# Shared expert weights in pieces of 256, 256 and 192 columns: the last 64 columns of gate and up as one chunk

## The chip, the cores and the metric

The kernel runs on one core of a Trainium2 chip. The metric is the device time of one execution in microseconds; three executions of the kernel before gave 2449.96, 2451.63 and 2456.68 us.

## The reference

A transformer block on 8192 tokens of 256 numbers (8 sequences of 1024), in float32:

```python
xn = _layernorm(x, axis=-1)
x = x + attention(xn) + ffn(xn)          # 16 heads of 16, ALiBi bias, softmax over the keys

# ffn: 8 experts of width 352, the best two of each token; one shared expert of width 704
h = jax.nn.silu(jnp.einsum('tc,ech->eth', xf, W1)) * jnp.einsum('tc,ech->eth', xf, W2)
y = jnp.einsum('eth,ehc,te->tc', h, W3, w)
hs = jax.nn.silu(xf @ Ws1) * (xf @ Ws2)
y = y.reshape(b, t, c) + (hs @ Ws3).reshape(b, t, c)
```

The shared expert is what the change is about: gate `xf @ Ws1` and up `xf @ Ws2`, each 256 to 704, their product `hs`, and down `hs @ Ws3`, 704 back to 256, for every token.

## The kernel before, in words

A float32 product is made of three matmuls on numbers split in a high part (rounded by a cast to fp32r) and a low part (what is left): low by high, high by low, high by high (`mm3`). All matmuls of this kind stand on one line, L497.

Each engine has a class (`Tensor`, `Scalar`, `Vector`, `Pool`, `Sync`) with the same methods, and `Order.run` calls them in one order for all. So the order of an engine is written out by hand, and engines meet at semaphores. The program has four stages: norm and projections; attention (with the routing, and transfers on POOL's queue that pack each expert's weights into a DRAM tensor `Wd`, `pack_expert`); 71 blocks (NBLK) of 256 routed rows, each with the weights of its expert; and 16 groups (NG) of 512 tokens with the shared expert, the attention's output projection and the sum of everything.

The shared expert is treated as two more experts of width 352. `pack_expert` packs them as experts 8 and 9, and `gather_weights` loads them as blocks 71 and 72 into one of three raw buffers WR (b % 3) with one transfer of 128 rows of 2176 numbers each. `split_block(b, i)` then splits three pieces of a set of weights: ACT casts all three to the high part (L806), POOL makes the low part of piece 0 (L1286), DVE that of pieces 1 and 2 (L1054). In a group, `shared_up(g, x, hc)` makes one of six chunks: two halves x of the width, each in chunks hc of 128, 128 and 96 columns. A chunk is 6 matmuls of gate and 6 of up, on PE, with 512 tokens as moving columns. Then ACT makes silu of gate (L848), DVE multiplies by up (`hf`, L1100), ACT casts that to the high part (`HH`, L854) and DVE makes the low part (`HL`, L1103).

A group's order on PE is: chunk 0, then the former group's `shared_down`, chunks 1, 2 and 3, the transposes of the next group's tokens (`group_columns`, L510; ACT and DVE turn them into high and low columns, L836 and L1083), chunks 4 and 5. `shared_down` has 24 matmuls of the attention's output with Wo and 72 on the six chunks, for four column blocks of 128 tokens. In the first group `shared_up(0, 0, 0)` stands before the last expert block's `block_down`, and the weights of the second half are split just behind it.

The waits that matter here: a gate chunk waits for the silu of the chunk two before it (`sg`), an up chunk for its product (`hf`), each chunk for the split weights (`wslp` by POOL, `wslv` by DVE) and for the group's columns (`sch`, `scl`). A load into WR[b % 3] waits until the set before in that buffer is split, a split into WB[b % 3] until the block before in it has done its down part (`down`).

Of the kernel before, what the change touches and what calls it, by code (L numbers as in the profile page):

```python
# [32 lines left out]
PIECES = ((0, W2_AT), (W2_AT, W3_AT), (W3_AT, RAW))  # L33
SCALE = float(HD) ** -0.5
# [43 lines left out]
class Order:  # L78
# [3 lines left out]
    def run(self):  # L82
# [96 lines left out]
        self.shared_up(0, 0, 0)  # L179
        self.block_down(NBLK - 1)  # L180
        for i in range(3):
            self.split_block(NBLK + 1, i)
        for j in range(4):
            self.gather_rows(0, j)
        for g in range(NG + 1):
            if 0 < g < NG:
                self.shared_up(g, 0, 0)
            if g >= 1:
                self.shared_down(g - 1)
            if g < NG:  # L190
                self.shared_up(g, 0, 1)
                self.o_columns(g)
                self.shared_up(g, 0, 2)
            if 1 <= g < NG:
                self.load_res(g)
                for j in range(4):
                    self.gather_rows(g, j)
            if g < NG:
                if g + 1 < NG:
                    self.load_o(g + 1)  # L200
                self.shared_up(g, 1, 0)
                if g + 1 < NG:
                    self.group_columns(g + 1)
                self.shared_up(g, 1, 1)
                self.shared_up(g, 1, 2)
                if g + 2 < NG:
                    self.load_rows(g + 2)
        self.end()

    def attention(self, s, n):  # L210
# [25 lines left out]
        if r % 2 == 0 and r // 2 < NE + 2 and kc == 1:  # L236
            self.pack_expert(r // 2)
# [65 lines left out]
    def shared_up(self, g, x, hc): pass  # L303
# [29 lines left out]
def up_index(g, x, hc):  # L333
    return NUP + 6 * g + 3 * x + hc


def build(nc, t, out):
    ctx = ExitStack()
    with ctx:
# [16 lines left out]
        Wd = dram("Wd", [(NE + 2) * P, RAW])  # L356
# [135 lines left out]
        class Tensor(Order):  # L492
# [194 lines left out]
            def shared_up(self, g, x, hc):  # L687
                h0, hn = HC[hc]
                n = up_index(g, x, hc)
                k, wt = (NBLK + g) % 2, WB[(NBLK + x) % 3]  # L690
                banks = 2 + 2 * (n % 2), 3 + 2 * (n % 2)
                self.w.wait_ge("sch", NBLK + g + 1)
# [5 lines left out]
                self.mm3(ps[0:hn, banks[0], :], self.operands(CH[:, k, :, :], CL[:, k, :, :], wt, h0, hn)  # L698
                         ).then_inc(sem["gmm"], 1)
                self.w.wait_ge("hf", n - 1)  # L700
                self.mm3(ps[0:hn, banks[1], :], self.operands(CH[:, k, :, :], CL[:, k, :, :], wt, W2_AT + h0, hn)
                         ).then_inc(sem["up"], 1)

            def shared_down(self, g):
                self.w.wait_ge("wslv", 2 * (NBLK + 2))
# [9 lines left out]
                for j in range(4):  # L715
                    col = slice(j * P, (j + 1) * P)
                    ks = []
                    for x in range(2):
                        wt = WB[(NBLK + x) % 3]
                        for hc in range(3):  # L720
                            n, hn, a = up_index(g, x, hc), HC[hc][1], W3_AT + hc * D
                            self.w.wait_ge("hh", n + 1)
                            self.w.wait_ge("hl", n + 1)
                            ks.append((HH[0:hn, n % 8, col], HL[0:hn, n % 8, col],
                                       wt[0:hn, a:a + D], wt[0:hn, RAW + a:RAW + a + D]))
                    self.mm3(ps[:, 6 + j // 2, (j % 2) * D:(j % 2) * D + D], ks, False, j % 2 == 1
                             ).then_inc(sem["sdn"], 1)


        class Scalar(Order):  # L730
# [65 lines left out]
            def split_block(self, b, i):  # L796
                if b > NBLK + 1:
                    return
                lo, hi = PIECES[i]
                self.w.wait_ge(f"wb{b % 3}", 16 * (b // 3 + 1))  # L800
                self.w.wait_ge("down", b - 2)
                if b in (1, 2):
                    self.w.wait_ge("acc1", NPAIR)
                    self.w.wait_ge("zero", 16 * NBLK)
                    self.w.wait_ge("wd", 80 * (NE + 2))
# [37 lines left out]
            def shared_up(self, g, x, hc):  # L843
                hn, n = HC[hc][1], up_index(g, x, hc)
                s, k = n % 8, n % 2
                self.w.wait_ge("hf", max(n - 1, NUP))
                self.w.wait_ge("gmm", n - NUP + 1)
                self.e.activation(sg[0:hn, k, :], ps[0:hn, 2 + 2 * (n % 2), :], ACT.Silu).then_inc(sem["sg"], 1)  # L848
# [5 lines left out]
                self.e.copy(HH[0:hn, s, :], hf[0:hn, k, :]).then_inc(sem["hh"], 1)  # L854


        class Vector(Order):
# [190 lines left out]
            def split_block(self, b, i):  # L1048
                if b > NBLK + 1 or i == 0:
                    return  # L1050
                lo, hi = PIECES[i]
# [40 lines left out]
            def shared_up(self, g, x, hc):  # L1092
                e = self.e
                hn, n = HC[hc][1], up_index(g, x, hc)
# [5 lines left out]
                e.tensor_tensor(hf[0:hn, k, :], ps[0:hn, 3 + 2 * (n % 2), :], sg[0:hn, k, :], ALU.mult  # L1100
                                ).then_inc(sem["hf"], 1)
                self.w.wait_ge("hh", n + 1)
                e.tensor_tensor(HL[0:hn, s, :], hf[0:hn, k, :], HH[0:hn, s, :].bitcast(F32),  # L1103
                                ALU.subtract).then_inc(sem["hl"], 1)
# [28 lines left out]
        class Pool(Order):  # L1133
# [89 lines left out]
            def pack_expert(self, x):  # L1223
                e = self.e
                if x < NE:
                    w1, w2, w3 = t["W1"][x], t["W2"][x], t["W3"][x]
                else:
                    a = (x - NE) * HE
                    w1, w2, w3 = t["Ws1"][:, a:a + HE], t["Ws2"][:, a:a + HE], t["Ws3"][a:a + HE, :]
# [34 lines left out]
            def gather_weights(self, b):  # L1264
                k = b % 3
                if b < NBLK:
                    self.w.wait_ge("rtw", 1)
                    self.w.wait_ge("wd", 80 * (NE + 2))
# [5 lines left out]
                else:  # L1274
                    e0 = (NE + b - NBLK) * P
                    self.w.wait_ge("wslp", b - 2)
                    self.w.wait_ge("wslv", 2 * (b - 2))
                    self.e.dma_start(WR[k][:, :], Wd[e0:e0 + P, :]).then_inc(sem[f"wb{k}"], 16)

            def split_block(self, b, i):  # L1280
                if b > NBLK + 1 or i != 0:
                    return
                lo, hi = PIECES[0]
# [22 lines left out]
            def shared_down(self, g):  # L1306
# [3 lines left out]
                self.w.wait_ge("hl", up_index(g + 1, 0, 0))  # L1310
# [213 lines left out]
```

## Time and profile before

| what | us |
|---|---|
| median of 3 executions | 2451.63 |
| lowest, highest | 2449.96, 2456.68 |
| the profiled execution | 2450.59 |
| its span | 2448.5 |
| busy in the span: PE, DVE, ACT, POOL | 2410.8, 2014.0, 1714.1, 1042.4 |
| first group's chunk 0 starts on PE at | 1975.13 |

Times of rows are microseconds from the start of the span. Between the profiled execution and its span lie 2.1 us outside the profile. PE is the matrix engine, DVE, ACT and POOL the vector, scalar and GpSimd engines, SP the queue that issues most transfers. A busy share counts instructions, and matmuls are pipelined, with modelled ends: the distance between the starts of two rows tells how fast they go, not their printed durations.

### The profile page before, as it was taken

To read this page: it belongs to the slowest core of one execution; us is meant where nothing else is said; L and a number is where in the kernel's file an instruction comes from. 1 tells how busy PE (TensorE), PEld (TensorE's weight loads), DVE (VectorE), ACT (ScalarE), POOL (GpSimd) and SP (SyncE) were. 2 spreads that over 40 slices of the span, in tenths; PEclk is the share of its full clock that TensorE was granted. 3 is DMA by queue.
4 is the path that set the end of the run, shared out by engine and by line. 5 is a ranking of instruction groups with operands and counts; after the bars stand their busy time and mean duration, and the time that the engine had idled before them with its cause. 6 is when DMAs were issued, how large, how long until landed. Compare 5 with 4: busy or idle time off the path is not lost.

```text
span 2448.5 us, 52126 instructions
## 1 busy us (share of the span) xinstructions
PE 2410.8 (98%) x20122; PEld 1605.7 (66%) x20122; DVE 2014.0 (82%) x3277; ACT 1714.1 (70%) x3274; POOL 1042.4 (43%) x994
## 2 busy tenths in 40 slices
PE   7999999999999999999999999999999999999999
PEld 5775444444444444444444448999999988888887
DVE  7987999999999999999999956777777765444444
ACT  4444888888889999998999997777777743332222
POOL 3332454544224545555455324333333334444444
PEclk9996999999999999999999999999999999999999
DMA  8994454544323444344443335777777744433332
GB/s 289 340 321 149 144 165 138 167 150 141 87 79 111 130 122 125 116 117 130 124 124 107 103 97 174 241 237 239 238 238 238 238 142 115 117 109 104 104 104 87
DMA packets 220263, 385.53 MB, mean 157 GB/s; under 512 B 53892, under 2 KB 141124, under 8 KB 210644
## 3 DMA queue, kind: packets, MB, share of 16 engines
q1 hardware_dynamic: 181744, 219.30, 29.2%
q0 software_dynamic: 37184, 162.09, 20.7%
q8 instruction: 160, 2.62, 0.5%
q10 hardware_dynamic: 1088, 0.79, 0.1%
q14 instruction: 87, 0.71, 0.1%
HBM read 250.15 MB, written 142.54 MB: 160 GB/s over the span
## 4 chain that ended last, share of the span: by engine, by line
PE 78%; DVE 18%; issue 3%; ACT 1%; DMA 0%; POOL 0%; DVEq 0%; SPq 0%; ACTq 0%; POOLq 0%
PE ps L497 76%; DVE mx L927 11%; DVE mx L930 4%; PE ps L510 2%; DVE qkL L917 0%; ACT qkH L767 0%; DVE xn L901 0%; DVE stats L866 0%; DMA xr<-Xn 0%; DMA xt<-in_x 0%; DVE XL L909 0%; POOL rstd L1155 0%; DVE mT L940 0%; DVE VB L1071 0%; ACT pta L782 0%
## 5 line engine op out<-in xcount | busy, mean ns | idle before, releaser
L927 DVE TENSOR_REDUCE mx<-ps 128x1 f32<-128x512 f32 x1560 | 964.7, 685 | 19.1 <-PE ps L497 17.7
L497 PE MATMUL ps<-OPS 54*128 54x512 f32 (+1 forms) x4096 | 792.0, 451 | 5.9 <-DVE mx L927 2.6
L497 PEld LDWEIGHTS ps<-OPS 54*128 54x128 f32 (+1 forms) x4096 | 388.6, 186 | 483.3 <-ACT pta L782 195.8
L782 ACT ACTIVATE pta<-ps 128x512 f32<-128x512 f32 x1024 | 541.5, 598 | 110.2 <-PE ps L497 104.7
L782 ACT ACTIVATE ptb<-ps 128x512 f32<-128x512 f32 x1024 | 538.8, 600 | 55.5 <-PE ps L497 48.2
L497 PE MATMUL ps<-OPS,WB 128*128 128x256 f32 (+1 forms) x2268 | 363.5, 312 | 2.9 <-DVE VB L1071 1.5
L497 PEld LDWEIGHTS ps<-OPS,WB 128*128 128x128 f32 x2268 | 310.6, 180 | 32.2 <-issue 3.3
L497 PE MATMUL ps<-pta,VB 128*32 128x352 f32 (+1 forms) x4096 | 304.1, 392 | 0.1
L497 PE MATMUL ps<-ptb,VB 128*32 128x352 f32 (+1 forms) x4096 | 302.4, 390 | 0.0
L930 DVE TENSOR_REDUCE mx<-ps 128x2 f32<-128x1024 f32 x244 | 297.8, 1220 | 0.0
L497 PE MATMUL ps<-OPS,WB0c 128*128 128x256 f32 (+3 forms) x1440 | 257.9, 331 | 2.9 <-DVE VB L1071 1.9
L497 PEld LDWEIGHTS ps<-OPS,WB0c 128*128 128x128 f32 (+1 forms) x1440 | 210.3, 181 | 32.9 <-issue 3.7
L1204 POOL TENSOR_SCALAR m<-m 128x16 f32<-128x16 f32 x64 | 19.3, 301 | 480.2 <-DVE m L934 480.2
L1216 POOL TENSOR_TENSOR sq<-sq,mone 128x16 f32<-128x16 f32 x64 | 190.1, 2971 | 69.4 <-DMA sq<-accs 68.8
L497 PE MATMUL ps<-WB,OPS 128*128 128x256 f32 (+1 forms) x1422 | 188.1, 283 | 0.0
L1076 DVE TENSOR_TENSOR OPS<-VB,OPS 128x256 fp32r<-128x256 f32 (+1 forms) x213 | 151.3, 710 | 33.6 <-ACT OPS L824 33.6
L848 ACT ACTIVATE VB<-ps 128x512 f32<-128x512 f32 (+1 forms) x96 | 57.0, 594 | 174.1 <-PE ps L497 174.1
L497 PEld LDWEIGHTS ps<-WB,OPS 128*128 128x128 f32 (+1 forms) x1422 | 178.4, 191 | 0.1
L497 PEld LDWEIGHTS ps<-ptb,VB 128*32 128x32 f32 x4096 | 94.2, 109 | 118.3 <-issue 116.7
L497 PEld LDWEIGHTS ps<-pta,VB 128*32 128x32 f32 x4096 | 94.2, 109 | 116.0 <-issue 100.2
L1260 POOL DMA_INDIRECT Xs<-xr,slot x128 | 131.1, 1024 | 59.3 <-PE ps L497 53.4
L854 ACT CAST OPS<-VB 128x512 fp32r<-128x512 f32 (+1 forms) x96 | 59.6, 621 | 138.2 <-DVE VB L1100 138.2
(155 smaller groups left out, 3003.1 us busy)
## 6 DMA issues: line engine op xcount, KB each, us to landing
OPS<-QKh SPq DMA_DIRECT2D x512, 64.0 KB
Xs<-zero POOLq DMA_DIRECT2D x71, 256.0 KB, 3.1
xr<-Xs SPq DMA_DIRECT2D x71, 256.0 KB, 5.3
Ys<-VB SPq DMA_DIRECT2D x71, 256.0 KB, 5.0
QKh<-qkH SPq DMA_DIRECT2D x16, 1024.0 KB, 7.2
QKl<-qkL SPq DMA_DIRECT2D x16, 1024.0 KB, 9.0
OPS<-QKl SPq DMA_DIRECT2D x256, 64.0 KB
asum<-Sd SPq DMA_DIRECT2D x64, 256.0 KB
```

What stands on the lines that cost most here:

```text
L497: return self.e.matmul(o, l, r, start=start, stop=stop)
L510: return self.e.transpose(o, in_, ident[:, :])
L782: self.e.activation(pt(m)[:, half * GT:(half + 1) * GT], ps[:, n % 3, :], ACT.Exp).then_inc(sem["exp"], 1)
L848: self.e.activation(sg[0:hn, k, :], ps[0:hn, 2 + 2 * (n % 2), :], ACT.Silu).then_inc(sem["sg"], 1)
L854: self.e.copy(HH[0:hn, s, :], hf[0:hn, k, :]).then_inc(sem["hh"], 1)
L927: self.e.reduce_max(mx[:, r % 2, hh, i, half:half + 1], ps[:, bank, :], AX.X).then_inc(sem["mxred"], 1)
L930: self.e.reduce_max(mx[:, r % 2, hh, i, :], ps[:, bank - 1:bank + 1, :], AX.X).then_inc(sem["mxred"], 2)
L1076: e.tensor_tensor(HL[0:hn, s, 0:BT], hfq[0:hn, k, :], HH[0:hn, s, 0:BT].bitcast(F32), ALU.subtract).then_inc(sem["hl"], 1)
L1204: e.tensor_scalar(m16[:, k2, :, :], m16[:, k2, :, :], -1.0, None, ALU.mult).then_inc(sem["mng"], 1)
L1216: self.e.tensor_tensor(sq[:, :], sq[:, :], mone[:, :], ALU.pow).then_inc(sem["rcp"], 1)
L1260: e.indirect_dma_start(Xs[:, :], bass.IndirectOffsetOnAxis(ap=slot[:, c, 4 * g + j:4 * g + j + 1], axis=0), xr[:, k, j, :], None).then_inc ...
```

## The change

The width 704 is no longer two halves of 352, but 256 + 256 + 192. There are five full chunks of 128 columns, and a sixth that holds the last 64 columns of gate in its rows 0 to 63 and the last 64 of up in rows 64 to 127, so that one set of 6 matmuls makes both. ACT's silu reads rows 0 to 63 and writes 64 to 127, where up and the product are. The sixth chunk's high part lies in rows 64 to 127 and its low part in rows 0 to 63 of one tile (`HH`), and down takes it with 2 matmuls instead of 3: against the low weights (zeros in rows 0 to 63), and against the high weights (the same 64 rows twice). The shared weights are now three sets, blocks 71, 72 and 73. They are not packed, but loaded from the inputs with 3, 3 and 7 transfers, and the third set is split behind the second.

```diff
+SX = 2 * D
+SHARED = (((0, SX), (SX, 2 * SX), (2 * SX, 3 * SX)), ((0, SX), (SX, 2 * SX), (2 * SX, 3 * SX)),
+          ((0, 4 * P), (4 * P, 6 * P), (6 * P, 10 * P)))
+SHARED_LOADS = (3, 3, 7)
...
-            if b + 3 <= NBLK + 1:
+            if b + 3 <= NBLK + 2:
                 self.gather_weights(b + 3)
...
-        self.shared_up(0, 0, 0)
+        self.shared_up(0, 0)
         self.block_down(NBLK - 1)
-        for i in range(3):
-            self.split_block(NBLK + 1, i)
+        for x in (1, 2):
+            for i in range(3):
+                self.split_block(NBLK + x, i)
...
-        if r % 2 == 0 and r // 2 < NE + 2 and kc == 1:
+        if r % 2 == 0 and r // 2 < NE and kc == 1:
             self.pack_expert(r // 2)
...
-        Wd = dram("Wd", [(NE + 2) * P, RAW])
+        Wd = dram("Wd", [NE * P, RAW])
...
+                at, up_at, step = ((j % 2) * P, SX + (j % 2) * P, D) if j < 4 else ((j - 4) * 4 * P, 2 * P, P)
...
+                if j == 1:
+                    self.w.wait_ge("hf", n - 1)
+                gate = self.mm3(ps[:, banks[0], :], self.shared_operands(xh, xl, wt, at, step))
+                if j == 5:
+                    gate.then_inc(sem["up"], 1)
+                else:
+                    gate.then_inc(sem["gmm"], 1)
+                    self.w.wait_ge("hf", n - 1)
+                    self.mm3(ps[:, banks[1], :], self.shared_operands(xh, xl, wt, up_at, step)).then_inc(sem["up"], 1)
...
             def shared_down(self, g):
-                self.w.wait_ge("wslv", 2 * (NBLK + 2))
+                self.w.wait_ge("wslv", 2 * (NBLK + 3))
...
+                    self.mm3(out_j, ks, False, False)
+                    n, wt, a = up_index(g, 5), WB[(NBLK + 2) % 3], 8 * P
+                    self.w.wait_ge("hh", n + 1)
+                    self.w.wait_ge("hl", n + 1)
+                    self.mm(out_j, HH[:, n % 8, col], wt[:, RAW + a:RAW + a + D], False, False)
+                    self.mm(out_j, HH[:, n % 8, col], wt[:, a:a + D], False, j % 2 == 1).then_inc(sem["sdn"], 1)
...
+                    self.w.wait_ge("up", n + 1)
+                    self.e.activation(sg[64:P, k, :], ps[0:64, bank, :], ACT.Silu).then_inc(sem["sg"], 1)
...
+                    self.e.copy(HH[64:P, s, :], hf[64:P, k, :]).then_inc(sem["hh"], 1)
...
+                if b == NBLK + 2 and i == 2:
+                    hi = 8 * P
+                    self.e.tensor_tensor(wt[64:P, RAW + hi:RAW + hi + D], WR[b % 3][64:P, hi:hi + D],
+                                         wt[64:P, hi:hi + D].bitcast(F32), ALU.subtract)
+                    self.e.tensor_scalar(wt[0:64, RAW + hi:RAW + hi + D], WR[b % 3][0:64, hi:hi + D], 0.0, None, ALU.mult)
...
+                    e.tensor_tensor(hf[64:P, k, :], ps[64:P, 2 + 2 * (n % 2), :], sg[64:P, k, :], ALU.mult
+                                    ).then_inc(sem["hf"], 1)
+                    self.w.wait_ge("hh", n + 1)
+                    e.tensor_tensor(HH[0:64, s, :], hf[64:P, k, :], HH[64:P, s, :].bitcast(F32), ALU.subtract
+                                    ).then_inc(sem["hl"], 1)
...
-                    self.e.dma_start(WR[k][:, :], Wd[e0:e0 + P, :]).then_inc(sem[f"wb{k}"], 16)
+                    w1, w2, w3, x, done = t["Ws1"], t["Ws2"], t["Ws3"], b - NBLK, sem[f"wb{k}"]
+                    parts = ((0, 2 * D, D, w1), (SX, 2 * D, D, w2)) if x < 2 else (
+                        (0, 2 * P, P, w1), (2 * P, 2 * P, P, w2), (4 * P, 2 * P, 64, w1), (4 * P + 64, 2 * P, 64, w2))
+                    for i, (at, size, width, w) in enumerate(parts):
+                        c0 = x * D if i < 2 else 5 * P
+                        lo = at if i < 2 else 4 * P
+                        self.e.dma_start(WR[k][:, lo:lo + size].rearrange("p (c n) -> p c n", c=2)
+                                         [:, :, at - lo:at - lo + width], rows(w[:, c0:c0 + width])).then_inc(done, 16)
+                    if x < 2:
+                        self.e.dma_start(WR[k][:, 2 * SX:3 * SX].rearrange("p (c n) -> p c n", c=2),
+                                         rows(w3[x * D:(x + 1) * D, :])).then_inc(done, 16)
+                    else:
+                        self.e.dma_start(WR[k][:, 6 * P:8 * P], w3[4 * P:5 * P, :]).then_inc(done, 16)
+                        for i in range(2):
+                            self.e.dma_start(WR[k][64 * i:64 * i + 64, 8 * P:10 * P], w3[5 * P:5 * P + 64, :]
+                                             ).then_inc(done, 16)
```

How the order changes on PE, in the first group from the last block's down part (WB1) to the attention's projections; WB2 and WB0c are the first and second set, WB1 the third. Before:

```order
L497 MATMUL ps<-WB1,OPS 128x256 x18
L497 MATMUL ps<-OPS,WB2 128x512 x12
L497 MATMUL ps<-OPS,WB2 96x512 x12
L497 MATMUL ps<-OPS,WB0c 128x512 x12
L510 MATMUL ps<-ident,xr 128x128 x8
L497 MATMUL ps<-OPS,WB0c 128x512 x12
L497 MATMUL ps<-OPS,WB0c 96x512 x12
```

Now:

```order
L511 MATMUL ps<-WB1,OPS 128x256 x18
L511 MATMUL ps<-OPS,WB2 128x512 x12
L511 MATMUL ps<-OPS,WB0c 128x512 x24
L524 MATMUL ps<-ident,xr 128x128 x8
L511 MATMUL ps<-OPS,WB1 128x512 x18
```

Chunk 2 belongs to the second set now, where it was the last chunk of the first; behind the transposes stand 18 matmuls instead of 24 up to the next group's chunk 0.

The same engine in `shared_down`, on the six chunks of a group (the last row is the next group's chunk 1). Before:

```order
L497 MATMUL ps<-WB2,OPS 128x256 x9
L497 MATMUL ps<-WB0c,OPS 128x256 x9
L497 MATMUL ps<-WB2,OPS 128x256 x9
L497 MATMUL ps<-WB0c,OPS 128x256 x9
L497 MATMUL ps<-WB2,OPS 128x256 x9
L497 MATMUL ps<-WB0c,OPS 128x256 x9
L497 MATMUL ps<-WB2,OPS 128x256 x9
L497 MATMUL ps<-WB0c,OPS 128x256 x9
L497 MATMUL ps<-OPS,WB2 128x512 x12
```

Now:

```order
L511 MATMUL ps<-WB2,OPS 128x256 x6
L511 MATMUL ps<-WB0c,OPS 128x256 x6
L511 MATMUL ps<-WB1,OPS 128x256 x5
L511 MATMUL ps<-WB2,OPS 128x256 x6
L511 MATMUL ps<-WB0c,OPS 128x256 x6
L511 MATMUL ps<-WB1,OPS 128x256 x5
L511 MATMUL ps<-WB2,OPS 128x256 x6
L511 MATMUL ps<-WB0c,OPS 128x256 x6
L511 MATMUL ps<-WB1,OPS 128x256 x5
L511 MATMUL ps<-WB2,OPS 128x256 x6
L511 MATMUL ps<-WB0c,OPS 128x256 x6
L511 MATMUL ps<-WB1,OPS 128x256 x5
```

Each of the four column blocks has 17 matmuls where it had 18.

DVE in the first group, from chunk 0's two steps over the splits to chunk 1's (WR0c and WR1c are the raw buffers of the second and the third set). Before:

```order
L1100 TENSOR_TENSOR VB<-ps,VB 128x512
L1103 TENSOR_TENSOR OPS<-VB,OPS 128x512
L1054 TENSOR_TENSOR WB0c<-WR0c,WB0c 128x704
L1054 TENSOR_TENSOR WB0c<-WR0c,WB0c 128x768
L1100 TENSOR_TENSOR VB<-ps,VB 128x512
```

Now:

```order
L1140 TENSOR_TENSOR VB<-ps,VB 128x512
L1142 TENSOR_TENSOR OPS<-VB,OPS 128x512
L1093 TENSOR_TENSOR WB0c<-WR0c,WB0c 128x512 x2
L1093 TENSOR_TENSOR WB1<-WR1c,WB1 128x256
L1090 TENSOR_TENSOR WB1<-WR1c,WB1 64x256
L1092 TENSOR_SCALAR WB1<-WR1c 64x256
L1093 TENSOR_TENSOR WB1<-WR1c,WB1 128x256
L1140 TENSOR_TENSOR VB<-ps,VB 128x512
```

Two operations between the steps of chunk 0 and of chunk 1 have become six.

## Rows read from the trace of the kernel before

**Rows 1.** The page's busy times: us, share of the span, instructions.

```profile
PE 2410.8 (98%) x20122; PEld 1605.7 (66%) x20122; DVE 2014.0 (82%) x3277; ACT 1714.1 (70%) x3274; POOL 1042.4 (43%) x994
```

**Rows 2.** Stretch in the shared stage: PE, PEld, DVE, ACT, POOL busy; PEclk, DMA share, GB/s.

```profile
2000.00:2100.00 100.00, 100.00 (x623) 87.73 (x623) 47.85 (x76) 27.21 (x43) 40.75 (x32) 1.00 0.36 95
```

**Rows 3.** The chain of waits: start, length, what. One group and the end.

```profile
2018.83 28.21 PE ps L497 x168
2047.04 0.87 PE ps L510 x8
...
2397.11 45.32 PE ps L497 x288
```

**Rows 4.** Timeline of PE: start, us, engine line op out<-in. One steady group.

```profile
2029.88 1.24 PE L497 MATMUL ps<-WB,OPS 128*128 128x256 f32 x9
...
2038.52 5.72 PE L497 MATMUL ps<-OPS,WB 128*128 128x512 f32 x24
2044.08 2.96 PE L497 MATMUL ps<-OPS,WB0c 128*128 128x512 f32 x12
2046.88 1.03 PE L510 MATMUL ps<-ident,xr 128*128 128x128 f32 x8
2047.67 5.82 PE L497 MATMUL ps<-OPS,WB0c 128*128 128x512 f32 x24
```

**Rows 5.** Groups on POOL in the attention stage: the packing transfers' issue, busy and mean ns.

```profile
L1231 POOL DMA_DIRECT2D Wd<-in_Ws x2 | 1.6, 804 | 0.0
...
L1235 POOL DMA_DIRECT2D Wd<-in_Ws x2 | 1.1, 562 | 0.0
```

**Rows 6.** Timeline of POOL around the first group: the splits.

```profile
1968.49 1.71 POOL L1286 TENSOR_TENSOR WB<-WR2c,WB 128x704 fp32r<-128x704 f32 x1 [4.63 <-ACT WB L806]
1981.74 1.71 POOL L1286 TENSOR_TENSOR WB0c<-WR0c,WB0c 128x704 fp32r<-128x704 f32 x1 [11.54 <-ACT WB0c L806]
```

**Rows 7.** DMA issues by tensor, whole run: count, KB each, median us to landing.

```profile
xr<-Xn SPq DMA_DIRECT2D x16, 512.0 KB, 11.3
...
Wd<-in_Ws POOLq DMA_DIRECT2D x4, 352.0 KB, 3.9
...
WR0c<-Wd POOLq DMA_DIRECT2D x1, 1088.0 KB, 5.6
```

**Rows 8.** Timeline of ACT in the first group: the three casts and what follows.

```profile
1980.88 2.20 ACT L806 CAST WB0c<-WR0c 128x704 fp32r<-128x704 f32 x3
1982.97 0.60 ACT L848 ACTIVATE VB<-ps 128x512 f32<-128x512 f32 x1
```

**Rows 9.** Timeline of PE in the first group: chunks 1 and 2.

```profile
1980.14 5.72 PE L497 MATMUL ps<-OPS,WB 128*128 128x512 f32 x24
```

**Rows 10.** The tile WR0c, 1940 to 2000 us: duration ns min/median/max on DVE.

```profile
L1054 DVE TENSOR_TENSOR WB0c<-WR0c,WB0c x5: 876/957/1830, 1939.6 to 1984.1; 128x768 fp32r<-128x768 f32 x3, 128x704 fp32r<-128x704 f32 x2
```

**Rows 11.** Timeline of DVE around the first group.

```profile
1961.39 0.41 DVE L1071 TENSOR_TENSOR VB<-ps,VB 128x256 f32<-128x256 f32 x1
...
1982.37 2.70 DVE L1054 TENSOR_TENSOR WB0c<-WR0c,WB0c 128x704 fp32r<-128x704 f32 x2 [2.04 <-ACT WB0c L806]
...
1992.71 1.23 DVE L1083 TENSOR_TENSOR OPS<-ps,OPS 128x1024 fp32r<-128x1024 f32 x1 [0.22 <-ACT OPS L836]
```

**Rows 12.** Timelines of DVE and ACT in a steady group: columns, a 96-row chunk.

```profile
2078.53 1.23 DVE L1083 TENSOR_TENSOR OPS<-ps,OPS 128x1024 fp32r<-128x1024 f32 x1 [0.22 <-ACT OPS L836]
...
2081.23 0.59 ACT L848 ACTIVATE VB<-ps 96x512 f32<-96x512 f32 x1
...
2082.68 0.69 DVE L1100 TENSOR_TENSOR VB<-ps,VB 96x512 f32<-96x512 f32 x1 [0.71 <-PE ps L497]
...
2083.40 0.62 ACT L854 CAST OPS<-VB 96x512 fp32r<-96x512 f32 x1 [1.58 <-DVE VB L1100]
...
2084.05 0.69 DVE L1103 TENSOR_TENSOR OPS<-VB,OPS 96x512 fp32r<-96x512 f32 x1 [0.69 <-ACT OPS L854]
```

**Rows 13.** The page's costliest groups: POOL's power on 128x16.

```profile
L1216 POOL TENSOR_TENSOR sq<-sq,mone 128x16 f32<-128x16 f32 x64 | 190.1, 2971 | 69.4 <-DMA sq<-accs 68.8
```

More of the change, by code:

```diff
@@ L190, in run @@
             if g < NG:
-                self.shared_up(g, 0, 1)
+                self.shared_up(g, 1)
                 self.o_columns(g)
-                self.shared_up(g, 0, 2)
+                self.shared_up(g, 2)
             if 1 <= g < NG:
@@ L330, in rows, with up_index, pieces, loads @@
     return w.rearrange("(c p) n -> p c n", p=P)
-def up_index(g, x, hc):
-    return NUP + 6 * g + 3 * x + hc
+def up_index(g, j):
+    return NUP + 6 * g + j
+def pieces(b):
+    return PIECES if b < NBLK else SHARED[b - NBLK]
+def loads(b):
+    return 16 * (b // 3 + 1) if b < NBLK else 16 * (b // 3 + SHARED_LOADS[b - NBLK])
 def build(nc, t, out):
@@ L697, in shared_up, with shared_operands @@
                 self.w.wait_ge("sg", n - 1)
[L698 to L702, printed above, removed]
+                if j == 1:
[7 more added lines that the diff above has]
+                    self.mm3(ps[:, banks[1], :], self.shared_operands(xh, xl, wt, up_at, step)).then_inc(sem["up"], 1)
+            def shared_operands(self, xh, xl, wt, at, step):
+                return [(wt[:, at + c * step:at + c * step + P], wt[:, RAW + at + c * step:RAW + at + c * step + P],
+                         xh[:, c, :], xl[:, c, :]) for c in range(2)]
             def shared_down(self, g):
-                self.w.wait_ge("wslv", 2 * (NBLK + 2))
+                self.w.wait_ge("wslv", 2 * (NBLK + 3))
                 self.w.wait_ge("yev", NBLK)
@@ L796, in split_block @@
             def split_block(self, b, i):
-                if b > NBLK + 1:
+                if b > NBLK + 2:
                     return
-                lo, hi = PIECES[i]
-                self.w.wait_ge(f"wb{b % 3}", 16 * (b // 3 + 1))
+                lo, hi = pieces(b)[i]
+                self.w.wait_ge(f"wb{b % 3}", loads(b))
                 self.w.wait_ge("down", b - 2)
@@ L841, in o_columns, with shared_up @@
                 self.e.copy(OH[:, :, :], orow[:, :, :]).then_inc(sem["och"], 1)
-            def shared_up(self, g, x, hc):
-                hn, n = HC[hc][1], up_index(g, x, hc)
-                s, k = n % 8, n % 2
+            def shared_up(self, g, j):
+                n = up_index(g, j)
+                s, k, bank = n % 8, n % 2, 2 + 2 * (n % 2)
                 self.w.wait_ge("hf", max(n - 1, NUP))
-                self.w.wait_ge("gmm", n - NUP + 1)
-                self.e.activation(sg[0:hn, k, :], ps[0:hn, 2 + 2 * (n % 2), :], ACT.Silu).then_inc(sem["sg"], 1)
+                if j < 5:
+                    self.w.wait_ge("gmm", 5 * g + j + 1)
+                    self.e.activation(sg[:, k, :], ps[:, bank, :], ACT.Silu).then_inc(sem["sg"], 1)
+                else:
+                    self.w.wait_ge("up", n + 1)
+                    self.e.activation(sg[64:P, k, :], ps[0:64, bank, :], ACT.Silu).then_inc(sem["sg"], 1)
                 if n - 8 >= NUP:
@@ L853, in shared_up @@
                 self.w.wait_ge("hf", n + 1)
-                self.e.copy(HH[0:hn, s, :], hf[0:hn, k, :]).then_inc(sem["hh"], 1)
+                if j < 5:
+                    self.e.copy(HH[:, s, :], hf[:, k, :]).then_inc(sem["hh"], 1)
+                else:
+                    self.e.copy(HH[64:P, s, :], hf[64:P, k, :]).then_inc(sem["hh"], 1)
         class Vector(Order):
@@ L1048, in split_block @@
             def split_block(self, b, i):
-                if b > NBLK + 1 or i == 0:
+                if b > NBLK + 2 or i == 0:
                     return
-                lo, hi = PIECES[i]
+                lo, hi = pieces(b)[i]
                 wt = WB[b % 3]
                 self.w.wait_ge("wsh", 3 * b + i + 1)
+                if b == NBLK + 2 and i == 2:
[3 more added lines that the diff above has]
+                    self.e.tensor_scalar(wt[0:64, RAW + hi:RAW + hi + D], WR[b % 3][0:64, hi:hi + D], 0.0, None, ALU.mult)
                 self.e.tensor_tensor(wt[:, RAW + lo:RAW + hi], WR[b % 3][:, lo:hi], wt[:, lo:hi].bitcast(F32),
```

65 lines of the change are left out of this document (29 added, 36 removed).

## The prediction

> **What bounds the kernel now.** I first read the busy times: PE is busy 98% of the span [rows 1]. Such a share says nothing about a stage, so I took the stretches next. From 2000 to 2100 us, inside the stage with the shared weights, PE is busy all 100.00 us at a granted clock of 1.00, DVE less than half of it [rows 2]. The chain of waits shows the same from the other side: it runs over PE alone, group after group, 28.21 us of matmuls and 0.87 us of transposes, and the last piece of PE is 45.32 us long [rows 3]. No other engine or transfer appears between them. So in this stage, 16 groups of 29.10 us, the time is the number of matmuls times the distance between their starts. What ends the stage, DVE's last sums and a store, is not touched.
>
> The distances come from the timeline of PE (its printed durations overlap, so I take differences of starts). 24 matmuls of 512 columns start at 2038.52 and the next 12 at 2044.08: 5.56/24 = 0.232 us each; those 12 take 2.80 us, 0.233 each. In the down part 72 of 256 columns fill the time from 2029.88 to 2038.52, 0.120 each [rows 4].
>
> **The change part by part.** *Gate and up.* Before, a group runs six chunks of 12 matmuls, 72. The order of the changed kernel has 12 + 24 + 30 = 66. The narrow chunks of 96 rows were as long as the full ones (the 24 at 2038.52 hold 12 of each kind), so fewer chunks is what counts. Gain 6 x 0.232 = 1.39 us a group.
>
> *Down.* Before 18 matmuls for each of four column blocks, now 6 + 6 + 5 = 17. Gain 4 x 0.120 = 0.48 us. Together 1.87 us a group, and 16 x 1.87 = **29.95 us**; a group should take 27.23.
>
> The Trainium skill, in TensorE: Matmul & The Clock Gate, section Back-to-back issue gap, gives the gap of an isolated matmul as N/2.4 + 2.5 ns. For these sizes that is an estimate of 216 and 109 ns, and the gain by it would be 16 x (6 x 0.216 + 4 x 0.109) = 27.7 us. The rows are 0.232 and 0.120, so this trace does not agree and I keep 29.95. The same section puts a stream of loads and matmuls at about 131 ns for N=512, which the rows do not bear out at all.
>
> *Packing.* The ten POOL transfers that copied the shared weights to DRAM during attention go. They cost POOL 0.80 to 0.56 us each [rows 5]. POOL is 43% busy and waits there; I take nothing, at most 0.5 us of gain.
>
> *Loads.* Instead of two transfers POOL issues 3 + 3 + 7. At the price of the packing transfers, the first two triples are issued in about 2.2 us each, and POOL was idle for over 4 us before its splits at that place (it started the one before the last at 1968.49) [rows 6]. The seven come behind that split: from about 1969.8, 7 x 0.65 = 4.6 us, to 1974.4. The nearest landings are 3.9 us for the packing and 11.3 us for the slowest kind of load [rows 7], so the last lands between 1978.3 and 1985.7. ACT asks for it after three copies, at about 1982.4. I take in time (it is nearest to the 3.9 of the same source); the other end is a delay of 3.3 us.
>
> *The splits, in group 0 only.* The third set of weights shares its buffer with the last expert block, so it is split after that block's down part, in front of chunk 1. ACT needed 2.09 us for 2176 columns, from 1980.88 to the activation at 1982.97 [rows 8]; for 2816 columns that is 2.70, or 0.6 late. Chunk 2 now belongs to the second set. PE reaches it at 1980.14 + 2.80 = 1982.94 [rows 9]. Its up half must be split by DVE, its gate half by POOL. DVE's split of 704 columns took 1.83 us while POOL's ran and 876 ns alone [rows 6, 10]. So DVE's first split of 512 columns ends about 0.65 us behind POOL's, which runs from 1981.4 for 512/704 x 1.71 = 1.24: at 1983.3. PE waits **0.4 us**. A second POOL split (1982.95 to 1984.2) holds DVE's next one to 1984.85, then four operations on 256 columns at 0.41 [rows 11], less 0.05 of overlap each: DVE is done at 1986.3. Before it was 1982.37 + 2.70 = 1985.07 [rows 11]. All DVE work behind it comes 1.2 us later, and the last of it that PE cannot hide is the low part of the next group's columns: 1992.71 + 1.23 = 1993.94 before [rows 11], 1995.1 now. PE wants it after chunk 1, the wait, chunks 2 and 3, the transposes (2047.67 - 2046.88 = 0.79 [rows 4]) and chunks 4 and 5: 1980.14 + 2.80 + 0.4 + 5.6 + 0.79 + 2.80 + 1.39 = 1993.9. That is a wait of about 1.15 us. Together **+1.5 us**. Ends: nothing, if DVE catches up, and 5 us with the late load. Later groups have the down part, in which DVE waits for PE, to recover.
>
> *Cover in every group.* Behind the transposes PE had 24 matmuls (5.6 us) before it needs the new columns, now 18 (4.2 us). In the group at 2047.67 [rows 4], one period on at 2076.77, DVE had them ready at 2078.53 + 1.23 = 2079.76 [rows 12], 3.0 us behind. So it stays hidden, with 1.2 us over. The short chunk's own steps on ACT and DVE take 0.59, 0.69, 0.62 and 0.69 us at 96 rows [rows 12], 2.6 in all; until its down part PE has 2.80 + 24 x 0.120 + 15 x 0.120 = 7.5 us, in the last group 4.7. Nothing.
>
> **Sum**: 2450.59 (the profiled execution) - 29.95 + 1.5 = 2422.1. The median shown is 1.04 higher, so **2423.2 us**.
>
> **The rivals.** *A, the cover breaks in each group.* If the new columns take more than 4.2 us instead of 3.0, PE waits in 15 groups. For it: ACT and DVE do them between two chunks, and the next chunk has half the matmuls. Against it: 1.2 us of slack, and DVE waits for PE between chunks. At 5.5 us the cost is 15 x 1.3 = 19.5: 2443.
>
> *B, the third set comes late.* Four of the seven transfers move runs of 512 or 256 bytes, and DMA is also loading rows, the attention's output and the residual then. If the last takes twice 11.3 us it lands at 1997.0; ACT's three copies and the activation of chunk 1 end 1.9 us later, and chunk 3, at 1986.1 on PE, waits for that activation: 13 us, 2436. Against it: these are 640 KB, where one of 1088 KB landed in 5.6 us [rows 7]. The Trainium skill, in DMA: Bandwidth & Descriptors, its opening table, wants at least 512 B per transfer for line rate and says that smaller ones are read, modified and written. That speaks against this change for its pieces of 64 columns; an estimate that doubles their time still hides them, and no row of this trace shows such a load.
>
> *C, slower than before: shifted partitions.* The short chunk's activation reads partitions 0 to 63 and writes 64 to 127, and DVE's low part goes back. No row shows such an operation on these engines. The nearest are the four of 96 rows, 0.6 to 0.7 us; the farthest is 2.97 us for POOL's small power [rows 13]. It decides at 7.5 + 1.87 = 9.4 us for the four, 2.3 us each, 3.6 times the rows; only from there does it eat the whole gain. At 2.97 us each they take 11.9, 4.4 over the cover in 15 groups and 7.2 in the last: 73 us on top of the forecast, 2496.
>
> *D, it does not do what it says.* Only if the removed matmuls were hidden. With PE at 100% and the chain on it they are not; the order shows 66 and 4 x 17. If the weight loads of what is left set the pace instead, the gain would about halve: 2438.
>
> **How the numbers follow.** Forecast 0.84, A 0.05, B 0.05, C 0.03, D 0.03. The forecast's own range: below, 31 us of gain with no wait and no late DVE, 2420.6, less 1 for the spread of executions (2449.96 to 2456.68 before); above, the late load at 5 us instead of 1.5, 2426.7, and 1.3 for that spread. So 2419.5 to 2428, which holds the forecast's 0.84 and none of the rivals. About 0.3% (7.4 us) is what a measurement of this kernel can tell from no change. A, B, D and the forecast are beyond it on the fast side, C mostly on the slow side; I leave 0.01 between.
>
> **What would show it.** Right: 27.23 us from one group's transposes to the next, 66 matmuls of 512 and 92 of 256 columns between, the same 0.232 and 0.120; a wait of PE of 0.4 us before chunk 2 of group 0 and of about 1.1 us before chunk 0 of group 1, released by DVE; no wait later. Wrong: a wait of PE in every group, on DVE's low columns (A) or on the short chunk's low part (C); ACT's copy of the third set released by a DMA (B); other distances between matmuls (D); or a change outside the last 490 us.

## The result, and the profile after

The changed kernel took 2418.67 us (median of 4 executions, 2417.59 to 2420.99) beside 2450.88 for the kernel before (2449.96 to 2456.68): 32.2 us less, a ratio of 0.9865 with a 95% interval of 0.9853 to 0.9876. The forecast was 2423.2 and its range ended at 2419.5: right in direction and in where the time goes, too small by 4.5 us, and outside the range. The profiled execution took 2417.59 us with a span of 2415.7, 32.8 less than before.

The page's busy times, which answer to [rows 1]:

```profile
PE 2375.3 (98%) x19962; PEld 1587.3 (66%) x19962; DVE 2020.4 (84%) x3281; ACT 1715.0 (71%) x3277; POOL 1042.2 (43%) x996
```

PE is still busy 98% of a shorter span. The chain of waits (start, length, what), as [rows 3]:

```profile
2018.26 26.04 PE ps L511 x158
2044.30 0.87 PE ps L524 x8
2045.17 26.04 PE ps L511 x158
...
2368.14 41.16 PE ps L511 x268
```

A group takes 26.04 + 0.87 = 26.91 us. It was 29.10, and 27.23 were forecast. PE is alone on the chain, so the stage has the same bound, and the time that the forecast did not have is inside the matmuls. The timeline of PE in one steady group, as [rows 4]:

```profile
2018.02 7.06 PE L511 MATMUL ps<-OPS,WB 128*128 128x512 f32 x30
2024.91 0.28 PE L511 MATMUL ps<-WoH,OL 128*128 128x256 f32 x1
...
2027.80 0.88 PE L511 MATMUL ps<-WB,OPS 128*128 128x256 f32 x6
...
2035.95 2.91 PE L511 MATMUL ps<-OPS,WB 128*128 128x512 f32 x12
2038.69 5.61 PE L511 MATMUL ps<-OPS,WB0c 128*128 128x512 f32 x24
2044.14 1.03 PE L524 MATMUL ps<-ident,xr 128*128 128x128 f32 x8
```

Down is as forecast: 68 matmuls from 2027.80 to 2035.95, 0.120 us each. Gate and up are not. 24 matmuls of 512 columns take 5.45 us from 2038.69 to 2044.14, 0.2271 each (23 of these distances are 226 or 227 ns, the last, to the transposes, is 232). Before, such 24 took 5.56. All 66 take 6.89 + 2.74 + 5.45 = 15.08 us, 0.2285 each. Before, all 72 had 29.10 - 0.79 of transposes - 2.87 (24 with Wo) - 8.64 (down) = 16.80, 0.2333 each. So besides the six matmuls that go, the 66 that stay are 0.0048 us shorter: 0.32 us a group, 5.1 us in 16.

The first group, timeline of PE (in brackets the idle time before, and who ended it):

```profile
1974.82 2.98 PE L511 MATMUL ps<-OPS,WB 128*128 128x512 f32 x12 [1.54 <-DVE VB L1110]
...
1983.18 5.73 PE L511 MATMUL ps<-OPS,WB0c 128*128 128x512 f32 x24 [0.48 <-issue]
1989.80 1.06 PE L524 MATMUL ps<-ident,xr 128*128 128x128 f32 x8 [0.90 <-DVE OL L1128]
1990.62 4.35 PE L511 MATMUL ps<-OPS,WB 128*128 128x512 f32 x18
1995.16 1.16 PE L511 MATMUL ps<-OPS,WB 128*128 128x512 f32 x4 [0.19 <-issue]
```

The idle times of the new waits sum to 1.57 us (the 1.54 before chunk 0 stood there before, too); what they cost PE comes to more, worked out below under the splits. And DVE and POOL there, which answer to [rows 11] and [rows 6]:

```profile
1981.70 3.07 DVE L1093 TENSOR_TENSOR WB0c<-WR0c,WB0c 128x512 fp32r<-128x512 f32 x2 [1.74 <-ACT WB0c L833]
...
1985.78 0.41 DVE L1093 TENSOR_TENSOR WB<-WR1c,WB 128x256 fp32r<-128x256 f32 x1
...
1993.84 1.22 DVE L1122 TENSOR_TENSOR OPS<-ps,OPS 128x1024 fp32r<-128x1024 f32 x1 [0.22 <-ACT OPS L863]
```

```profile
1981.23 1.29 POOL L1340 TENSOR_TENSOR WB0c<-WR0c,WB0c 128x512 fp32r<-128x512 f32 x1 [7.55 <-ACT WB0c L833]
1982.78 1.44 POOL L1340 TENSOR_TENSOR WB<-WR1c,WB 128x512 fp32r<-128x512 f32 x1 [0.26 <-ACT WB L833]
```

DVE's two splits of 512 columns took 3.07 us while POOL's two ran; an earlier one of the same shape, with POOL idle, took 0.68 (1974.48). Nothing else moved much: the shared stage starts 0.31 us earlier, and the tail behind the last matmul is 0.3 us longer.

### The profile page after: what moved, and what is told of

Same layout as the page of the kernel before. It is cut to its first block, busy times and chain, and to the rows that moved or that the text cites. A ratio compares the mean times of both kernels' runs of the same rounds, so it can differ in the third digit from the quotient of the medians.

```text
span 2415.7 us, 51818 instructions
## 1 busy us (share of the span) xinstructions
PE 2375.3 (98%) x19962; PEld 1587.3 (66%) x19962; DVE 2020.4 (84%) x3281; ACT 1715.0 (71%) x3277; POOL 1042.2 (43%) x996
## 4 chain that ended last, share of the span: by engine, by line
PE 77%; DVE 18%; issue 3%; ACT 1%; DMA 1%; POOL 0%; SPq 0%; DVEq 0%; ACTq 0%; POOLq 0%
PE ps L511 75%; DVE mx L961 11%; DVE mx L964 4%; PE ps L524 2%; DVE xn L935 0%; DVE stats L900 0%; DMA xr<-Xn 0%; DMA xt<-in_x 0%; SPq L1436 0%; POOL rstd L1199 0%; DVE qkL L951 0%; DMA OPS<-Alid 0%; DVE XL L943 0%; ACT qkH L794 0%; DVE WB0c L1093 0%
## 5 line engine op out<-in xcount | busy, mean ns | idle before, releaser
L511 PE MATMUL ps<-OPS,WB 128*128 128x256 f32 (+2 forms) x2364 | 384.6, 315 | 3.1 <-DVE VB L1110 1.5
L511 PEld LDWEIGHTS ps<-OPS,WB 128*128 128x128 f32 (+1 forms) x2364 | 332.3, 182 | 28.3 <-issue 3.9
L511 PE MATMUL ps<-OPS,WB0c 128*128 128x256 f32 (+2 forms) x1248 | 206.4, 317 | 3.4 <-issue 2.5
L511 PE MATMUL ps<-WB,OPS 128*128 128x256 f32 (+1 forms) x1550 | 206.1, 283 | 0.0
L511 PEld LDWEIGHTS ps<-WB,OPS 128*128 128x128 f32 (+1 forms) x1550 | 194.8, 191 | 0.1
L511 PEld LDWEIGHTS ps<-OPS,WB0c 128*128 128x128 f32 (+1 forms) x1248 | 178.9, 183 | 19.5 <-issue 3.7
L876 ACT ACTIVATE VB<-ps 128x512 f32<-128x512 f32 x80 | 47.6, 595 | 160.4 <-PE ps L511 160.0
L1356 POOL DMA_INDIRECT gath<-Ys,slot x128 | 130.5, 1019 | 36.5 <-issue 35.0
```

Source lines behind the costliest of these rows:

```text
L511: return self.e.matmul(o, l, r, start=start, stop=stop)
L876: self.e.activation(sg[:, k, :], ps[:, bank, :], ACT.Silu).then_inc(sem["sg"], 1)
L1356: self.e.indirect_dma_start(gath[:, j, c, :], None, Ys[:, :], bass.IndirectOffsetOnAxis(ap=slot[:, c, i:i + 1], axis=0)).then_inc(sem[f"ga ...
```

## Why the matmuls that stay became faster: the experiments

Two differences between the kernels touch the matmuls of 512 columns that stay. Theory W: the kernel before had chunks of 96 columns, the changed one has none. Theory A: the kernel before read its weights at steps of c * 352 columns, 1408 bytes, which is 5.5 times 256; the changed one reads them at multiples of 512 bytes. Every kernel below was timed beside the kernel before on the same chip: wide96, step384, step224 and twice5 beside one set of its runs (2451.3), wide384, step192, pad32 and later_split beside another (2451.56), pad64, down18 and padxh beside a third on another chip (2451.7), w3off beside a fourth (2453.24). The changed kernel's 2418.67 comes from runs of its own, so a difference of one or two microseconds from it says little; there the rows decide.

### wide96: the narrow chunks made wide

```diff
-                self.mm3(ps[0:hn, banks[0], :], self.operands(CH[:, k, :, :], CL[:, k, :, :], wt, h0, hn)
+                self.mm3(ps[:, banks[0], :], self.operands(CH[:, k, :, :], CL[:, k, :, :], wt, h0, P)
```

and the same for up.

> The kernel before, but the 96-column chunks of gate and up are 128 wide on PE alone (the 32 further columns are other weights; ACT and DVE read rows 0 to 95 as before, so nothing in the result changes). Same 72 matmuls a group. Theory W (loads of 96 columns are what keeps the matmuls of 512 columns at 0.2335 us instead of 0.2285): the group's period falls from 29.10 to about 28.74 us, the kernel is about 5.3 us faster than before. Theory A (the places of the weights, c * 352 columns, are what matters): period 29.10, time unchanged within 1 us. A third, that the number of semaphore steps or chunks matters: unchanged too.

2450.12 us, ratio 0.9999 (0.9989 to 1.0008). Its chain has the 28.21 of the kernel before:

```profile
2105.38 28.21 PE ps L497 x168
```

Period 29.09 with the transposes. Theory W falls as the main cause.

### step384 and wide384: the kernel before, with the weights at other places

```diff
-                return [(wt[:, at + c * HE:at + c * HE + hn], wt[:, RAW + at + c * HE:RAW + at + c * HE + hn],
+                return [(wt[:, at + c * step:at + c * step + hn], wt[:, RAW + at + c * step:RAW + at + c * step + hn],
```

with step 384 for the shared chunks, and 768 in place of W2_AT. wide384 has the edit of wide96 as well.

> The kernel before, with the weights of gate and up in the shared stage read at steps of 384 columns instead of 352 and the up part at 768 instead of 704, so that each slice of weights begins at a multiple of 512 bytes of its set. The numbers multiplied are then partly other weights; matmuls, sizes and waits are the same. Theory A: matmuls of 512 columns at 0.227 to 0.2285 us, period about 28.7, the kernel 5 to 6 us faster than before. Theory W: 0.2335 and 29.10 us, unchanged.

> The kernel before with both: slices at steps of 384 columns and up at 768 (other weights are multiplied), and the third chunks 128 columns wide. With steps alone the full chunks ran at 0.228 and the chunks of 96 at 0.2304 us. If the width matters only once the places are right, all run at 0.2272: period 28.65 (after 29.10 before and 28.87 with the steps alone), about 7 us faster than before. If the 0.2304 has another cause, 28.87.

step384: 2446.69 us, ratio 0.9980 (0.9970 to 0.9989). wide384: 2446.78, ratio 0.9982 (0.9972 to 0.9991). The chain of each:

```profile
2106.78 27.99 PE ps L497 x168
```

```profile
2109.72 27.87 PE ps L497 x168
```

The places alone take 0.23 us off a group (28.86 to 28.87 with the transposes), the width another 0.12, and only once the places are right. Against 28.21 that is 0.34 us for 72 matmuls, 0.0048 each: what the changed kernel gained on each of its 66. The forecast for wide384 was 28.65, it came to 28.74. The places take 3.7 us off 16 groups; the times fell by 4.6, with an interval of 2.7 to 7.4 (0.0011 to 0.0030 of 2451).

### step224 and step192: the changed kernel, with one slice moved

```diff
-                at, up_at, step = ((j % 2) * P, SX + (j % 2) * P, D) if j < 4 else ((j - 4) * 4 * P, 2 * P, P)
+                at, up_at, step = ((j % 2) * P, SX + (j % 2) * P, D - 32) if j < 4 else ((j - 4) * 4 * P, 2 * P, P - 32)
```

step192 has 64 in place of 32.

> The changed kernel, with the second slice of each pair of weights (c = 1) 32 columns, 128 bytes, before its place, in gate and up of the shared stage. The numbers multiplied are then partly other weights; matmuls, sizes and waits are those of the changed kernel. Theory A: the matmuls of 512 columns go back from 0.2285 to about 0.233 us, the period from 26.91 to about 27.2 us, 4 to 5 us slower than the changed kernel. Theory W: 26.91 us and unchanged.

> The changed kernel with the second slice of each pair of weights (c = 1) 64 columns, 256 bytes, before its place, in gate and up of the shared stage (other weights, same matmuls, sizes and waits). If all slices only need the same place modulo 256 bytes, the matmuls of 512 columns stay at 0.2272 us and the period at 26.91. If they need it modulo 512, they go to about 0.232 and the period to 27.2, as with 128 bytes.

step224: 2421.36 us (2420.01 to 2423.03), 2.7 us over the changed kernel's median; step192: 2419.11. The chain of step224, then of step192:

```profile
2100.75 26.36 PE ps L511 x158
```

```profile
2099.88 26.04 PE ps L511 x158
```

128 bytes off cost 0.32 us a group, and the period is 27.23, exactly the forecast's. That is 5.1 us in 16 groups; the times show 2.7, less than the 4 to 5 expected, and their ranges overlap (the changed kernel's ends at 2420.99), so it is the rows that show it. 256 bytes off cost nothing. So the forecast's period was that of a changed kernel whose weights lie as badly as before.

### pad32 and pad64: the sets moved against the moving columns

```diff
         gath = sbuf(C, "gath", [P, 4, 2, D])
+        sbuf(C, "pad32", [P, 32])
         WB += [sbuf(C, f"WB{i}", [P, 2 * RAW], F32R) for i in (1, 2)]
```

pad64 leaves 64 columns free. By the tile sizes, WB0c begins 49152 + 32768 + 16384 + 3 x 8704 = 124416 bytes behind OPS, in which the moving columns lie: 486 times 256. WB1 and WB2 are multiples of 256 too, until a pad moves them.

> The changed kernel with 32 columns (128 bytes) left free before WB1 and WB2 in on-chip memory, so that the sets WB1 and WB2 lie 128 bytes off against the moving columns (OPS) and against WB0c; within a set all slices keep their place to each other. If the place of the weights against that of the moving columns is what counts (theory M), matmuls on WB1 and WB2 go to about 0.232 us and those on WB0c stay at 0.2267: 42 of the 66 matmuls, period about 27.1, 3.4 us slower than the changed kernel. If the place of one slice against the next counts (theory N), all stay at 0.227, 26.91 us, apart from one or two matmuls where the set changes.

> The control of pad32: 64 columns (256 bytes) free before WB1 and WB2 instead of 32. If what counts is the place of the weights against the moving columns modulo 256 bytes, all matmuls of 512 columns stay at 0.2272 us and the period at 26.91. If it is the distance itself, or the other buffers that move, matmuls on WB1 and WB2 go to 0.232 as with 128 bytes.

The timeline of PE in pad32, one group:

```profile
2103.47 7.22 PE L512 MATMUL ps<-OPS,WB 128*128 128x512 f32 x30
2110.53 0.28 PE L512 MATMUL ps<-WoH,OL 128*128 128x256 f32 x1
...
2121.46 2.94 PE L512 MATMUL ps<-OPS,WB 128*128 128x512 f32 x12
2124.24 5.61 PE L512 MATMUL ps<-OPS,WB0c 128*128 128x512 f32 x24
2129.69 1.03 PE L525 MATMUL ps<-ident,xr 128*128 128x128 f32 x8
```

The 42 matmuls on the moved sets are slower, 2110.53 - 2103.47 = 7.06 and 2.78 us where the changed kernel has 6.89 and 2.74. The 24 on WB0c keep their 5.45. The period is 27.00 instead of the 27.1 expected, since down took 0.1 us less at the same time (8.06 us from 2113.40 to 2121.46, where the changed kernel has 8.15). In pad64 it is back:

```profile
2106.44 26.04 PE ps L512 x158
```

So one slice against the next (theory N) does not explain it: within the moved sets no slice moved against another, and they are slower. Nor is it the distance itself, but the place of the weights modulo 256 bytes (theory M). The times, 2420.11 and 2419.99 us, do not tell the two apart; the rows do. Two limits of this. The moving columns stood still in both runs, so these alone do not show that the place counts against them; padxh below moves the columns instead. And there is no fixed price for each badly placed matmul: in pad32 all 42 on the moved sets are off and lose (0.17 + 0.04)/42 = 0.005 us each, while in step224 only every second slice is off, and the mean loss of all 66 is the same 0.32/66 = 0.005.

### twice5 and down18: each term of the sum undone

```diff
                 if j == 5:
+                    gate = self.mm3(ps[:, banks[0], :], self.shared_operands(xh, xl, wt, at, step))
                     gate.then_inc(sem["up"], 1)
```

```diff
                     self.mm(out_j, HH[:, n % 8, col], wt[:, RAW + a:RAW + a + D], False, False)
+                    self.mm(out_j, HH[:, n % 8, col], wt[:, RAW + a:RAW + a + D], False, False)
```

> The changed kernel with the six matmuls of the short chunk made twice (the second time over the first, the same numbers), so 72 matmuls of 512 columns a group as before. This undoes the gate and up term alone. At 0.227 us each the period grows by 1.36 us, 16 groups by 21.8 us: about 2440.5. By the prediction's 0.232 it would be 22.3. If the removed matmuls had been partly hidden, less than 18.

> The changed kernel with the short chunk's matmul against the low weights made twice in down (that small part is then added twice, so down has 18 matmuls a column block as before). This undoes the down term alone: 4 x 0.120 = 0.48 us a group, period 27.39, 16 x 0.48 = 7.7 us slower than the changed kernel, about 2426.3. If these matmuls had been hidden, the period stays at 26.91.

twice5: 2438.82 us (2438.53 to 2439.54). down18: 2427.09 (2425.09 to 2431.09). The chains:

```profile
2104.62 27.40 PE ps L511 x164
```

```profile
2100.75 26.52 PE ps L511 x162
```

1.36 and 0.48 us a group, as expected. In time 20.2 and 8.4 us, where 21.8 and 7.7 were expected. None of these matmuls is hidden. 1.36 + 0.48 = 1.84 us, of the 2.19 that a group gained, is the count; the rest is the place and the width.

### later_split: the third set split behind chunk 1

```diff
-        for x in (1, 2):
-            for i in range(3):
-                self.split_block(NBLK + x, i)
+        for i in range(3):
+            self.split_block(NBLK + 1, i)
...
                 self.shared_up(g, 1)
+                if g == 0:
+                    for i in range(3):
+                        self.split_block(NBLK + 2, i)
```

(the first gathers of rows move along).

> The changed kernel with the third set's splits moved behind chunk 1 of group 0 (ACT, DVE and POOL make them between chunk 1 and the attention's output). PE's wait of 0.48 us before chunk 2 stays, since it is the second set's; the waits of 0.90 (transposes) and 0.19 us (chunk 0 of group 1) shrink: together 0.5 to 1.1 us faster than the changed kernel, about 2417.9. That is less than the spread of executions; the profile must show it. If the third set comes late for chunk 4 instead, PE waits there and nothing is gained.

2418.96 us (2418.32 to 2420.44), the changed kernel's time. The timeline of PE:

```profile
1983.99 5.72 PE L513 MATMUL ps<-OPS,WB0c 128*128 128x512 f32 x24 [0.48 <-issue]
1990.54 1.06 PE L526 MATMUL ps<-ident,xr 128*128 128x128 f32 x8 [0.82 <-DVE OL L1130]
```

The wait moves from 0.90 to 0.82 us and the 0.19 behind it stays. DVE does the same work ahead of `OL`, on which the transposes wait, whether the splits stand before chunk 1's steps or behind them. The expectation missed that; a split later still (not tried) would meet chunk 4, which needs it.

### padxh: the moving columns moved, in the projections

```diff
+        sbuf(A, "padxh", [P, 48])
         XH, XL = (sbuf(A, n, [P, 2, 2, GT], F32R) for n in ("XH", "XL"))
```

> The changed kernel with 192 bytes free before XH and XL, the moving columns of the projections. They lay 64 bytes off modulo 256 against the weights Wh and Wl, and the 384 matmuls of 512 columns of that stage ran at 0.2303 us. If the same rule holds there, they go to 0.227: 384 x 0.0033 = 1.3 us off the 380 us of the projections as far as PE sets their end, about 1 us faster than the changed kernel. If 64 bytes off do not count, or the moving columns of another tile do not obey it, 0.2303 stays and the time too.

2421.44 us (2418.4 to 2423.71): no gain. The groups of PE up to 210 us, of the changed kernel and of padxh (busy, mean ns):

```profile
L511 PE MATMUL ps<-XL,Wh 128*128 128x512 f32 x128 | 51.0, 398 | 0.0
```

```profile
L512 PE MATMUL ps<-XL,Wh 128*128 128x512 f32 x128 | 51.1, 399 | 0.0
```

But the single distances did change, and they show the rule at work. In the first groups 17 of these matmuls follow each other without a wait. The last ten of them in one such group, first and last start, of the changed kernel and of padxh:

```profile
44.39 0.39 PE L511 MATMUL ps<-XL,Wh 128*128 128x512 f32 x1
...
46.45 0.39 PE L511 MATMUL ps<-XL,Wh 128*128 128x512 f32 x1
```

```profile
44.40 0.39 PE L512 MATMUL ps<-XL,Wh 128*128 128x512 f32 x1
...
46.44 0.39 PE L512 MATMUL ps<-XL,Wh 128*128 128x512 f32 x1
```

Nine distances take 2.06 us in the one, 2.04 in the other. To the nanosecond the trace has 226, 229 and 232 in turn in the changed kernel (mean 229), 64 bytes off, and 226 and 227 in padxh, the steady value of the shared stage. The same holds for each of the four such groups from 31.8 to 75 us, and every other kernel of this document has the changed kernel's pattern there, within two nanoseconds. In this stage the weights stood still and the columns moved (with the buffers behind them, which PE does not read there): the place of the one against the other counts. (A run that moves both by the same amount was not made.)

Why nothing was gained: the steady value comes only after some seven matmuls, and the first ones of a stretch are slower in padxh (231, 231, 236, then 240 and 235 in later groups). From 98 us on the stretches are 12 and 6 long. Those of 12 took 2.98 us in padxh, on average of nine, and 2.96 in the changed kernel; those of 6 took 1.53 in both. So the placing pays in long stretches such as the shared stage's 66, not in short ones.

### w3off: the down weights 128 bytes off

Down's weights are the moving side, and in pad32 its matmuls had gained. The edit adds 32 columns to the place of the third piece in each set (`2 * SX + 32` and `6 * P + 32` where it is loaded, split and read).

> The changed kernel with the down weights (moving columns there) kept 32 columns (128 bytes) further in each shared set, at 0.232's distance against the stationary HH; the result is the reference's. In pad32 the 256-column matmuls of down went from 0.1199 to 0.1185 us while those of 512 columns lost. If the 128 bytes help short matmuls by themselves, 68 x 0.0014 = 0.09 us a group: period 26.82, 1.5 us faster in the profile, less than a comparison of times can tell. If the gain in pad32 came from the gate and up matmuls beside it, 26.91. If the rule of gate and up held for these too, slower.

2418.34 us (2416.55 to 2420.82), beside 2418.67. The chain:

```profile
2099.10 25.97 PE ps L511 x158
```

0.07 us a group, 1.1 us in 16, near the 0.09 expected. For matmuls of 256 columns the badly placed weights are the slightly better ones. It is the fastest version by its rows, but its ratio of 0.9862 (0.9845 to 0.9878) beside the changed kernel's 0.9865 does not tell the two apart.

## Why the prediction was wrong, point by point

**The step that failed** is the one that sizes the change's first two terms, "The distances come from the timeline of PE", with what the prediction would see after: "the same 0.232 and 0.120". It priced what goes at its measured distance, correctly (twice5: 1.36 us a group where 1.39 stood), and took for granted that the 66 that stay keep theirs. They went from 0.2333 to 0.2285 us. The sum has no term for them. The new layout of the weights was read for what it packs, not for where each slice lies. 16 x 0.32 = 5.1 us is more than the whole miss of 4.5. step224 puts the layout's error back and gives the forecast's period of 27.23.

**The range** had no place for it either. Its lower end, "31 us of gain", was the sum without waits and one more microsecond. The distances were taken as known from both sides, because rows showed them; but they belonged to another layout. An honest bound was in the rows: 24 matmuls at 2038.52 held single steps from 0.224 to 0.240 us, so something disturbed them, and the nearest floor was the shortest.

**The page's distance.** The prediction set aside its estimate of 216 ns for 512 columns (by the formula for an isolated matmul in the Trainium skill, TensorE: Matmul & The Clock Gate, Back-to-back issue gap). The best steady distance here is 0.2267 us, still 11 ns above it. What the comparison could have told is that 0.2333 might have room beneath it.

**Down**: 0.48 us a group, confirmed by down18.

**Packing**: nothing forecast, 0.31 us earlier at the start of the shared stage, within what executions differ by (1974.41 in wide96, 1976.72 in step384).

**Loads and rival B**: the last of the seven was issued by 1973.7 (forecast 1974.4), the small ones landed in 6.7 us by the DMA view, so at about 1980.4, between the two ends. ACT cast the third set from 1982.09 on (forecast 1982.4) without a wait.

```profile
WR1c<-in_Ws POOLq DMA_DIRECT2D x4, 64.0 KB, 6.7
```

**The splits in group 0**: +1.5 us forecast, 0.48 + 0.90 + 0.19 = 1.57 of idle time measured, but some 2.1 lost. The idle time is counted from a matmul's modelled end, which lies behind the start that an undisturbed next one would have had. From chunk 0 to behind the transposes stand 74 instructions in both kernels; they took 1990.62 - 1974.82 = 15.80 us, and before, by the starts of these rows, 14.37:

```profile
1975.13 3.03 PE L497 MATMUL ps<-OPS,WB 128*128 128x512 f32 x12 [1.54 <-DVE VB L1071]
...
1989.50 5.81 PE L497 MATMUL ps<-OPS,WB0c 128*128 128x512 f32 x24
```

With the 0.2 us that their 48 matmuls of 512 columns should have gained, that is 1.6 lost. Group 1, with the wait of 0.19, took 27.40 (1990.62 to 2018.02) and not 26.91, 0.5 more. So the forecast's size is 0.6 short, and its agreement with the 1.57 is luck. The place is half right: the larger wait stands before the transposes, for `OL`, not before chunk 0 of group 1. The working followed DVE's queue to the low columns and passed `OL`, on which `group_columns` waits (`ocl`). DVE was done with the splits at 1986.19 (forecast 1986.3). Behind the price lay POOL's split that holds DVE's; the Trainium skill (SBUF — State Buffer, Who interferes with whom) calls the port they share an exclusive lock, and here two splits took 3.07 us beside two of POOL, 1.98 in later_split beside one.

**Cover (rival A)**: DVE had the columns ready at 2046.69 + 1.22 = 2047.91, 2.98 us behind chunk 4's start at 2044.93 (forecast 3.0, cover 4.1). No wait in any later group.

**Rival C**: the operations across partitions cost what others do. ACT and DVE on the short chunk (timeline; the first row of ACT and the last of DVE go across):

```profile
2049.38 0.59 ACT L879 ACTIVATE VB<-ps 64x512 f32<-64x512 f32 x1
...
2050.84 0.62 ACT L888 CAST OPS<-VB 64x512 fp32r<-64x512 f32 x1 [0.87 <-issue]
```

```profile
2050.11 0.70 DVE L1144 TENSOR_TENSOR VB<-ps,VB 64x512 f32<-64x512 f32 x1
2051.49 0.69 DVE L1147 TENSOR_TENSOR OPS<-VB,OPS 64x512 fp32r<-64x512 f32 x1 [0.68 <-issue]
```

**Rival D**: out; twice5 and down18 show every removed matmul on the path.

The sum with the measured sizes: 16 x 2.19 = 35.0, less 2.1 of waits, plus 0.3 of an earlier start, less 0.3 of a longer tail: 32.9 against 32.8 in the profiled spans. Against the forecast: 5.1 more from the matmuls that stay, 0.6 less from the waits, which is the 4.5 missed.

## What to carry to other kernels

When a change moves operands in memory, price the instructions that stay as well as those that go: where PE is the bound, 5 ns on each of a thousand matmuls is 5 us. Look at single distances, not at their mean: a steady 0.2267 is undisturbed, 0.224 to 0.241 is not, and what is above the steady value is a bound for what a change of layout may give. Where weights and moving columns are packed by hand, a step such as 352 is worth rounding up, but time it in its own stage: in the projections, with stretches of 6 and 12, it gave nothing.

## What the runs showed of the hardware

- A matmul of 128 x 128 weights on 512 columns (fp32r) started every 0.2267 us where the weights lay at the place of the moving columns modulo 256 bytes, and about every 0.232 where half of the slices (step224) or all of them (pad32) were 128 bytes off. 256 bytes off: no loss. The granted clock was 1.00 there. In the projections 64 bytes off gave 0.229, and moving the columns to the weights' place gave 0.2267, after some seven matmuls of a stretch (padxh).
- The first matmuls of a phase are disturbed in any case: 12 right behind down took 2.74 us (0.2283), the next 24 took 5.45 (0.2271).
- Weight slices of 96 columns instead of 128 made the matmul no faster; with good places 72 of them, 24 being narrow, took 0.12 us longer a group (step384 against wide384).
- With 256 moving columns it is the other way round: 0.07 us a group less with the moving weights 128 bytes off (w3off).
- Why the place counts was not shown. No row here names a memory port of PE.
